# Attention and mixture-of-experts block, start of the expert layers: seven weight subtractions move to GpSimd, two transposed inputs move into the last attention group, the second layer runs three tiles behind the first

## The reference

```python
x = L0_attn_x                                # 4 x 1024 x 256
mod = silu(c) @ wmod                         # sa, ca, ga, sb, cb, gb for each batch entry
h = layernorm(x) * (1 + ca) + sa
x = x + ga * attention(h)                    # 16 heads of 16, causal, fp32 softmax
h = layernorm(x) * (1 + cb) + sb
logits = h @ gate_w                          # 8 experts, the best 2 of each token
y_e = silu(h @ w1[e]) @ w2[e]                # 256 -> 512 -> 256
x = x + gb * sum(weight_e * y_e over the token's 2 experts)
```

## Time and profile before

| | us |
|---|---|
| median of 3 runs | 979.91 |
| lowest, highest | 978.81, 981.2 |
| the profiled execution | 980.17 |
| its span | 978.5 |
| mean granted clock of PE | 0.979 of full speed |
| busy: PE, DVE, ACT, POOL | 892.9, 707.1, 580.1, 388.3 |

### The profile page before, as it was taken

One profiled execution on the slowest core, in us unless ns is written; L12 is line 12 of the kernel. 1 busy time (PEld: TensorE's weight loads), 2 busy tenths in 40 slices (PEclk: granted clock), 3 DMA queues, 4 the chain that ended last, 5 costly groups with the idle time before them and its releaser, 6 DMA issues.

```text
span 978.5 us, 19384 instructions
## 1 busy us (share of the span) xinstructions
PE 892.9 (91%) x6164; PEld 529.8 (54%) x6164; DVE 707.1 (72%) x2285; ACT 580.1 (59%) x1268; POOL 388.3 (40%) x386
## 2 busy tenths in 40 slices
PE   7898999998999999999999988888999999999990
PEld 4453444443535434544443543432799899999980
DVE  7887777779566889656789678899447575444587
ACT  3365477766776668496677658767435433333563
POOL 4203101741531435433234354135486465555630
PEclk9999999999999999999999999999899999999995
DMA  6487536534506537235275573116332323222699
GB/s 209 120 177 173 69 84 98 79 94 77 79 26 123 90 94 152 55 47 122 51 120 118 118 168 127 36 27 205 85 98 77 97 77 103 76 77 75 213 299 308
DMA packets 83596, 110.62 MB, mean 113 GB/s; under 512 B 16290, under 2 KB 56794, under 8 KB 83498
## 3 DMA queue, kind: packets, MB, share of 16 engines
q1 hardware_dynamic: 73194, 84.22, 36.5%
q0 software_dynamic: 9216, 22.80, 9.2%
q10 hardware_dynamic: 1088, 2.36, 0.7%
HBM read 69.42 MB, written 35.41 MB: 107 GB/s over the span
## 4 chain that ended last, share of the span: by engine, by line
PE 68%; DVE 16%; ACT 5%; issue 4%; DMA 3%; POOL 2%; SPq 1%; DVEq 0%; ACTq 0%; POOLq 0%
PE PO L1756 11%; PE PS L1736 10%; PE PH L1623 9%; PE PM L1713 9%; PE PY L1623 9%; PE PHT L1841 3%; PE PX L1768 3%; DVE MXF L1426 2%; PE PX L1688 2%; ACT PR L1089 2%; PE PX L1692 2%; PE PX L1677 2%; DVE JK L1423 2%; PE PS L1740 2%; DMA YG<-YT 1%
## 5 line engine op out<-in xcount | busy, mean ns | idle before, releaser
L1089 ACT ACTIVATE PR<-PS 128x512 f32<-128x512 f32 (+3 forms) x768 | 334.7, 497 | 126.0 <-PE PS L1740 91.9
L1423 DVE CUSTOM_DVE_ANT_0 JK<-PM,MK 128x128 bf16<-128x128 f32 (+3 forms) x512 | 238.4, 483 | 51.0 <-PE PM L1713 50.5
L1713 PE MATMUL PM<-QK 128*128 128x512 bf16 (+3 forms) x768 | 246.5, 331 | 23.1 <-DVE MXF L1426 12.5
L1736 PE MATMUL PS<-QK 128*128 128x512 bf16 (+3 forms) x768 | 245.7, 331 | 10.0 <-ACT PR L1089 9.1
L1426 DVE TENSOR_REDUCE MXF<-PM 128x1 f32<-128x512 f32 x256 | 175.0, 684 | 75.2 <-PE PM L1713 73.5
L1736 PEld LDWEIGHTS PS<-QK 128*128 128x128 bf16 x768 | 75.2, 98 | 166.0 <-ACT PR L1089 106.4
L1756 PE MATMUL PO<-PR,V 128*17 128x512 f32 (+3 forms) x1536 | 161.3, 492 | 0.0
L1713 PEld LDWEIGHTS PM<-QK 128*128 128x128 bf16 x768 | 75.0, 98 | 98.9 <-DVE MXF L1426 33.4
L1623 PE MATMUL PY<-W2S,HT 128*128 x852 | 119.3, 289 | 2.8 <-issue 1.9
L1623 PE MATMUL PH<-W1S,XT 128*128 x426 | 114.5, 405 | 0.7 <-DVE W2S L1578 0.7
L1740 PE MATMUL PS<-MT,identb 128*128 128x128 bf16 x512 | 111.4, 220 | 0.0
(11 more groups left out here) (284 smaller groups left out, 1203.6 us busy)
## 6 DMA issues: line engine op xcount, KB each, us to landing
QK<-SD SPq DMA_DIRECT2D x180, 128.0 KB
SD<-SP SPq DMA_DIRECT2D x42, 256.0 KB, 3.3
LP<-LR SPq DMA_DIRECT2D x64, 64.0 KB, 2.3
W1S<-in_w SPq DMA_DIRECT2D x8, 512.0 KB, 7.0
OP<-OS POOLq DMA_DIRECT2D x60, 64.0 KB, 6.5
X<-XA SPq DMA_DIRECT2D x3, 1024.0 KB, 11.2
H2D<-XA SPq DMA_DIRECT2D x3, 1024.0 KB, 4.9
YG<-YT SPq DMA_DIRECT2D x12, 256.0 KB, 5.1
```

Source lines behind the costliest of these rows:

```text
L1089: eng.activation(PR[:, slot, i, c0:512], PS[m % 3][:, c0:512], ACT.Exp, scale=0.25).then_inc(S["exp"].sem, 1)
L1423: eng.tensor_tensor_reduce(JK[:, jk % 2, 0:w], PM[m % 3][:, 0:w], MK[:, 512 - w:512], 1.0, -3.0e38, ALU.add, ALU.max, MXA[:, mb, h, qt:qt ...
L1713: eng.matmul(PM[m % 3][:, 0:128 * (k1 - k0)], QK[:, r, h, 0, qt * 128:(qt + 1) * 128], QK[:, r, h, 1, k0 * 128:k1 * 128], start=True, stop ...
L1736: last = eng.matmul(PS[m % 3][:, c0:512], QK[:, r, h, 1, j * 128:(j + 1) * 128], QK[:, r, h, 0, 512 * f + c0:512 * f + 512], start=True, s ...
```

## The change

It does four things.

1. **low**: the seven subtractions for experts 0, 3, 4, 5, 6, 7 and 1 go from DVE to POOL, and from group 15's window (slots 10 to 19) to the windows of groups 13 and 14, each one step behind the next expert's `split`. Expert 2, whose weights come last, stays on DVE.
2. **turnx(0), turnx(1)**: both go ahead of the last two `pv` steps; tile 1's transposes use the bank `PH[1]` and no longer wait for tile 0's low part. The load of tile 0's expert number moves with them.
3. **cut, rest**: those of experts 4 to 6 go ahead of `up(0)`, and those of expert 7 from behind `up(1)` to behind `up(0)`.
4. **down**: runs three tiles behind `up`, and ahead of `turnh` in its turn; `ystore` runs four behind.

```diff
-    for n, e in enumerate((0, 3, 4, 5, 6, 7, 1, 2)):
-        place(NG - 1, 10 + 1.5 * n, one("low", e))
+    for n, e in enumerate((0, 3, 4, 5, 6, 7, 1)):
+        place(NG - 3, 17 + 3 * n, one("low", e))
+    place(NG - 1, 20, one("low", 2))
...
+    for t in range(2):
+        place(NG - 1, 23.5, one("turnx", t))
...
-    early = {0: [("rest", 5), ("cut", 6)], 1: [("rest", 6), ("cut", 7), ("rest", 7)]}
-    order += [("wload", 1, 7), ("od", NG - 1), ("turnx", 0), ("xload", 3), ("cut", 4), ("turnx", 1), ("xload", 4), ("rest", 4), ("cut", 5)]
+    early = {0: [("cut", 7), ("rest", 7)]}
+    order += [("wload", 1, 7), ("od", NG - 1), ("xload", 3), ("xload", 4), ("cut", 4), ("rest", 4), ("cut", 5), ("rest", 5), ("cut", 6), ("rest", 6)]
...
-        if 0 <= t - 3 < NF:
-            order.append(("ystore", t - 3))
+        if 0 <= t - 4 < NF:
+            order.append(("ystore", t - 4))
...
+        if 0 <= t - 3 < NF:
+            order.append(("down", t - 3))
         if 0 <= t - 1 < NF:
             order.append(("turnh", t - 1))
         order += early.get(t, [])
-        if 0 <= t - 2 < NF:
-            order.append(("down", t - 2))
...
+        def turned_in(t):
+
+            return PH[1][:, 0:256].rearrange("p (k n) -> p k n", k=2) if t == 1 else PXT[:, 0:2, :]
...
+                elif kind == "low" and a[0] != 2:
+                    e = a[0]
+                    po.wait_ge(*after("sp_a", "split", e))
+                    turn("lo_p")
+                    eng.tensor_tensor(W1L[:, e], W1L[:, e].bitcast(F32), W1H[:, e].bitcast(F32), ALU.subtract).then_inc(S["lo_p"].sem, 1)
...
                     else:
-                        ac.wait_ge(*after("pv", "pv", NG - 1, 1, 7))
-                    eng.activation(XT[:, t % 2, 0, :, :], PXT[:, 0:2, :], ACT.Copy).then_inc(S["xhi"].sem, 1)
+                        ac.wait_ge(*after("pv", "pv", NG - 1, 1, 5))
+                    eng.activation(XT[:, t % 2, 0, :, :], turned_in(t), ACT.Copy).then_inc(S["xhi"].sem, 1)
...
-                    if t >= 1:
+                    if t >= 2:
                         pe.wait_ge(*after("xlo", "turnx", t - 1))
...
+                    if t == 0:
+                        expert[0] = expert_of(0)
...
                     pe.wait_ge(*after("xlo", "turnx", t))
-                    pe.wait_ge(S["sp_d"], S["sp_d"].before["cut", 0])
+                    pe.wait_ge(*after("sp_d", "low", 2))
+                    pe.wait_ge(*after("lo_p", "low", 1))
```

More of the change, by code:

```diff
@@ L401 @@
     "rest": {"sp_d": 1},
-    "low": {"sp_d": lambda e: 1 + int(e == 2)},
+    "low": {"sp_d": lambda e: 2 * int(e == 2), "lo_p": lambda e: int(e != 2)},
     "xload": {"xl0": lambda t: 16 * (t % 3 == 0), "xl1": lambda t: 16 * (t % 3 == 1), "xl2": lambda t: 16 * (t % 3 == 2)},
@@ L546, in adaln_block @@
         W2H, W2L = W2S[:, :, 0, :, :], W2S[:, :, 1, :, :]
+        sb("PAD2", [128, 128], F32, ffn)
         XT = sb("XT", [128, 2, 2, 2, 128], FR, ffn)
@@ L550, in adaln_block @@
         YO = sb("YO", [128, 4, D], F32, ffn)
-        sb("PAD1", [128, D], F32, ffn)
+        sb("PAD1", [128, 128], F32, ffn)
         XL = sb("XL", [128, 3, D], F32, ffn)
@@ L882, in gpsimd_program @@
             const = S["const"].sem
-            done = {n: 0 for n in ("const", "sub_p", "neg_p", "gbo", "div_p", "om", "bias", "h2", "both")}
+            done = {n: 0 for n in ("const", "sub_p", "neg_p", "gbo", "div_p", "om", "bias", "h2", "lo_p", "both")}
             newest = []
@@ L1563, in vector_program @@
                         eng.tensor_scalar(TE[:, ts], TE[:, ts], E - 1, None, ALU.bitwise_and).then_inc(tb.sem, 1)
-                elif kind == "low":
+                elif kind == "low" and a[0] == 2:
                     e, c = a[0], S["sp_d"].before[step]
[L1566 to L1571, removed]
+                    dv.wait_ge(S["w02"], 16)
+                    eng.tensor_copy(W1H[:, e], W1L[:, e].bitcast(F32)).then_inc(S["sp_d"].sem, 1)
+                    dv.wait_ge(S["sp_d"], c + 1)
                     eng.tensor_tensor(W1L[:, e], W1L[:, e].bitcast(F32), W1H[:, e].bitcast(F32), ALU.subtract).then_inc(S["sp_d"].sem, 1)
@@ L1585, in vector_program @@
                     dv.wait_ge(*after("xhi", *step))
-                    eng.tensor_tensor(XT[:, t % 2, 1, :, :], PXT[:, 0:2, :], XT[:, t % 2, 0, :, :].bitcast(F32),
+                    eng.tensor_tensor(XT[:, t % 2, 1, :, :], turned_in(t), XT[:, t % 2, 0, :, :].bitcast(F32),
                                       ALU.subtract).then_inc(S["xlo"].sem, 1)
@@ L1818, in tensor_program @@
                         pe.wait_ge(*after("mx", "max", NG - 1, NM - 1))
-                    eng.transpose(PXT[:, 0, :], XL[:, t % 3, 0:128], ident[:, :])
-                    eng.transpose(PXT[:, 1, :], XL[:, t % 3, 128:256], ident[:, :]).then_inc(S["fx"].sem, 1)
+                    eng.transpose(turned_in(t)[:, 0, :], XL[:, t % 3, 0:128], ident[:, :])
+                    eng.transpose(turned_in(t)[:, 1, :], XL[:, t % 3, 128:256], ident[:, :]).then_inc(S["fx"].sem, 1)
+                    if t == 0:
+                        expert[0] = expert_of(0)
                 elif kind == "up":
                     t = a[0]
-                    if t == 0:
-                        expert[0] = expert_of(0)
                     pe.wait_ge(*after("xlo", "turnx", t))
-                    pe.wait_ge(S["sp_d"], S["sp_d"].before["cut", 0])
+                    pe.wait_ge(*after("sp_d", "low", 2))
+                    pe.wait_ge(*after("lo_p", "low", 1))
                     if t >= 2:
```

## The result

The changed kernel takes 987.67 us in the median of 8 runs (984.81 to 991.21), the kernel before beside it 980.56 (976.75 to 987.23): ratio 1.0064, 95% interval 1.0037 to 1.0091. It is slower. The profiled execution took 985.51 us, with a span of 983.8, against 980.17 and 978.5.

What follows compares the result with a forecast made beforehand. It took DVE's routing and maxima between 617 and 640 to bound the kernel there: 980.17 + 5.4 - 2.6 = 983.0, so 982.8 expected in the median. Its own range was 980.3 to 985.6, the whole range 977.2 to 986.0.

Steps and rivals of the forecast that it cites:

- the first mechanism: In attention's routing, a small DVE operation reading two SBUF operands waits until POOL's 2.36 us operation ends, delaying DVE's queue.
- 0.6, 2.1, 1.7 and 1.5: Predicted holds, in us, of DVE's routing by POOL's subtractions for experts 5, 6, 7 and 1; sum 5.9.
- +5.4: Attention's loss from POOL holding DVE: 5.9 us of holds, with 0.46 of DVE idle time; bounds 4.0 and 7.0.
- down three behind: In the expert tiles, running down three tiles behind up leaves PE's 3.48 us per tile unchanged; cost nothing.
- 2.2 for PE: At the start of the expert layers, PE's work gets ahead by 2.2 us; bounds 1.3 and 3.0.
- 3.6 for the first `out`: At the start of the expert layers, the first out runs about 703.6, 3.6 us earlier.
- The `recip` term: At the expert layers' start, recip on DVE could run about 690.6, 2.7 us earlier, without casts before it.
- The division: Ahead of the first out, the division, which stood behind an input load on POOL, may gain nothing to 1.5 us.
- -2.6 for the whole start and end: Gain in us taken for the start of the expert layers and the last gathers, which start 2.2 to 3.6 earlier.
- that rival's 1.6: At the end, the third tile of distance shrinks the 2.6 us gain to 1; time 984.5, chance 0.06.
- a hole ... in the tiles past 730: A sign in the profile after that would show the forecast wrong, as would a hole before down.
- The loss is larger: Rival: PE's clock falls after DVE's holds in attention, losing up to 1.7 us per stretch; 986, chance 0.12.

Runs made afterwards that it cites:

- low_only: The kernel before with only the seven low subtractions moved to POOL at their new places; 991.55 us, ratio 1.0073 to the kernel before.
- low_back: The changed kernel with the low subtractions back on DVE at their old places; 987.87 us, ratio 1.0024 to the kernel before.
- one_input: The changed kernel with each POOL subtraction replaced by a same-size multiplication by a constant, reading one operand; 986.20 us, ratio 1.0044 to the kernel before.
- order_only: The kernel before with only down three tiles behind up and ahead of turnh, ystore four behind; 989.78 us, ratio 1.0046.
- halves: The changed kernel with each POOL subtraction split into two of 128x512; 987.40 us, ratio 1.0075 to the kernel before.
- order_back: The changed kernel with down two tiles behind again and turnh ahead of down; 989.01 us, ratio 1.0039 to the kernel before.
- between: The changed kernel, down still three behind, with batch entry 3's steps between down and turnh; 984.09 us, ratio 1.0032 to the kernel before.
- start_only: The kernel before with only the new start of the expert layers, low steps and down as before; 977.83 us, ratio 0.9963 to the kernel before.

## Why the prediction was wrong

**The sign and the first mechanism were right.** It said that "a small DVE operation that reads two SBUF operands waits until POOL's operation is over": the four holds came at the four subtractions named, 0.5, 1.8, 2.1 and 1.2 us against 0.6, 2.1, 1.7 and 1.5, and the loss at the last copy was 5.7 against +5.4. That these two are so near is partly luck: 5.1 of it is measured around three of the holds, 0.4 is the early transposes' (put at 0.6), and the profile had been 1.0 ahead at 543. low_only and low_back confirm the mechanism. The class of operation was drawn too narrowly: a `CAST` and a `TENSOR_SCALAR` that read one operand (617.40 and 626.94) were held as well.

The Trainium skill's SBUF — State Buffer, under "Who interferes with whom", has cast and `tensor_scalar` in 2-port modes and `tensor_tensor` with two SBUF inputs contend with GpSimd, and `tensor_reduce` never. The changed kernel's trace agrees on each: 0.67, 1.98 and 1.58 us held, and 0.34 not; whether the first two ran in such a mode no view shows. It also says that the second one blocks until the first finishes; that holds for the subtractions, and one_input's hold of 0.69 us inside an operation of 2.78 doesn't fit it, nor do its unheld `TENSOR_TENSOR` at 619.09.

**The failed step is "down three behind".** The prediction said: "the order of its parts leaves no operand late, since each has more distance than before. Nothing." It costs 3.6 us between tiles 15 and 25 (6.8 in order_only and in low_back). The argument looked at the tile's own operands, and was right on those. It didn't look at what stands behind the moved step in the queues of ACT and DVE: batch entry 3's logits, four times, and its routing. The price is worked out from the rows: three waits that are longer by 0.43 each and one by 0.9, 2.2 together, and 1.6 for the 4 us at a clock of 0.60. halves measures the same two parts, 2.1 and 1.6. order_only and order_back show that the order makes it, between that the neighbour does.

**The start was sized too small.** The prediction took 2.2 for PE and 3.6 for the first `out`; measured from the last copy are 4.2 (5.60 less the product owed) and 5.6, of which some 0.4 only makes up for the copy that the early transposes delay. The `recip` term was right, 2.9 against 2.7: it stands 9.2 us behind the last copy to `OS` instead of 12.1. The division was put at 0 to 1.5, and came 2.0 closer to `recip` (8.7 instead of 10.7), and `out` followed it 0.6 closer. The rounds of DMA were not shorter: SP issues its last ones until 6.7 us behind `recip` before and 6.5 after. What shrank is the time from there to the division, 4.0 to 2.2. Before, the division starts directly behind an input load that POOL issues at 703.04; after, POOL waits 0.88 us for the DMA. So the input load in POOL's queue was the right thing to name, and 1.5 was too small a bound. In start_only, without `down` three behind, the gain at tile 5 was 5.1 and none of it was owed. PE stood idle behind `up(1)`, as the prediction had it, but until 692.66 and for tile 3's input, not for the first silu, which ran at 690.79.

**The end.** "-2.6 for the whole start and end" lumped two things. The gain at the start is not lost on the way: 25 to 70 is within 0.4. At the end the third tile of distance costs 0.4 on top of the product that it owes, less than that rival's 1.6.

So 5.4 - 2.6 = +2.8 became 5.7 - 4.2 + 3.6 + 0.4 and -0.2 of small terms, +5.3 in the profiles. With the 3.6 at nothing it would have been +1.7, inside the forecast's own range. (The upper end of that range comes to 985.5 by its own terms, not 985.6, and the 3.6 and 1.4 in its two ends are worked out nowhere.) The timed sum of the parts agrees: +0.73% for the `low` steps and +0.46% for the order, -0.37% for the start, together +0.82% against 0.64% measured, inside the intervals. Taken out of the changed kernel instead, the `low` steps are worth 0.40% and the order 0.25%; so the timing alone sizes each only to within a factor of two.

The prediction named its own refutation, "a hole ... in the tiles past 730", and that is what came. "The loss is larger" had a clock that falls after the held stretch; where it fell most was at 777, after the routing's wait.

## What to carry to other kernels

A step that is moved in a static order has two neighbours in each engine's queue: check what now stands directly behind it and is waited for, not only whether its own operands are ready. Work given to an idle POOL is not free when DVE has small SBUF operations on the path; look for the nearest DVE operation that overlapped a POOL one, and note its kind. And a change of several parts can hide a gain: here the part with the casts' order was worth having alone (0.3 to 0.4%).

## What the runs showed of the hardware

A POOL subtraction of 2.36 us held DVE's `CAST` (0.67 us), `TENSOR_SCALAR` (up to 2.29) and `TENSOR_TENSOR` (1.58), and not `TENSOR_REDUCE` (0.34). Three holds of 5.09 us together moved the next copy to `OS` by 5.09. Halving POOL's operation did not halve the hold: 2.11 us over two back-to-back operations of 1.29 and 1.26. A multiplication with one operand took POOL longer, 2.78 instead of 2.36 us, and held DVE for less, two times ending in its middle.

A PE wait of 2.2 us in the changed kernel and one of 1.3 in order_only were each followed by a stretch of 4 us at a mean clock of 0.60 and 0.70, mostly the 1.2 GHz level; one of 1.3 in the kernel before and one of 2.2 in halves were not.
